# Preparing the second attention's first batch inside the layer before it, and another order for the first two token tiles of the last layer

## The reference, cut to what matters

```python
# second cross-attention: q from the normalised x, k and v from the context
attn = jnp.einsum('bct,bcs->bts', qh * scale, kh * scale)   # 8 heads of 64 channels
attn = jax.nn.softmax(attn, axis=-1)
out = jnp.einsum('bts,bcs->bct', attn, vh)
# FFN1: every operand is rounded to fp8 in blocks of 32 with one scale a block
gate = _mx_linear(x2d, gate_w); up = _mx_linear(x2d, up_w)
h = jax.nn.silu(gate) * up            # then rounded again, times down_w
```

## Time and profile before

| what | value |
|---|---|
| median of 3 runs | 1505.21 us (1503.46 to 1505.53) |
| the profiled execution | 1497.97 us |
| its span, first to last instruction | 1496.2 us |
| mean granted TensorE clock | 0.930 |
| PE busy | 1294.4 us (87%) |
| DVE busy | 1168.2 us (78%) |
| ACT busy | 659.3 us (44%) |
| POOL busy | 475.3 us (32%) |

### The profile page before, as it was taken

How to read it: one execution, slowest core, us unless ns; L and a number is a source line. 1 busy time by engine, 2 the same in 40 slices (tenths; PEclk the granted TensorE clock), 3 DMA queues, 4 the chain that set the end, 5 groups by cost and what they waited for, 6 DMA issues and landing times. The chain is left out here.

```text
span 1496.2 us, 20180 instructions
## 1 busy us (share of the span) xinstructions
PE 1294.4 (87%) x7472; PEld 649.8 (43%) x7496; DVE 1168.2 (78%) x1554; ACT 659.3 (44%) x1047; POOL 475.3 (32%) x344
## 2 busy tenths in 40 slices
PE   4589999466998899985787888889999999999998
PEld 3268777331444444442122222334444444444444
DVE  5557787875888788894868768788888878888885
ACT  3345666255554455433555545233343344433322
POOL 0031431365566566641458697200000000000000
PEclk8879999555999999998799999999999999999999
DMA  8412123237434252234001003130000000000000
GB/s 298 152 62 68 31 99 99 90 120 211 149 120 132 88 155 85 85 127 168 30 6 51 15 16 112 53 117 8 7 14 7 7 7 7 7 7 7 14 8 15
DMA packets 59734, 106.77 MB, mean 71 GB/s; under 512 B 10879, under 2 KB 21783, under 8 KB 59532
## 3 DMA queue, kind: packets, MB, share of 16 engines
q1 hardware_dynamic: 58380, 101.60, 21.0%
q0 software_dynamic: 1280, 4.20, 1.0%
HBM read 73.73 MB, written 27.66 MB: 68 GB/s over the span
## 5 line engine op out<-in xcount | busy, mean ns | idle before, releaser
L1697 PE MATMUL FD<-W0D,HH 128*128 128x512 f16 x512 | 156.2, 387 | 7.7 <-DVE ROOM L1756 3.4
L2597 PE MATMUL HD<-W1H,HT 128*128 128x512 f16 x480 | 145.2, 379 | 0.0
L335 ACT ACTIVATE DD<-E,TM 128x128 f32<-128x128 f32 x256 | 72.7, 369 | 69.6 <-PE E L431 68.0
L1691 PE MATMUL FG<-F,W0G 97*128 97x512 f16 x324 | 82.2, 384 | 20.8 <-PEq L1036 11.6
L1622 POOL TENSOR_TENSOR HL<-ROOM,HH 128x512 f16<-128x512 f32 x48 | 76.1, 1585 | 74.9 <-ACT HH L1651 74.9
L1697 PE MATMUL FD<-W0D,HL 128*128 128x512 f16 x256 | 98.8, 386 | 0.0
L2359 DVE TENSOR_REDUCE NQ<-A_M 128x2 f32<-128x1024 f32 x60 | 73.3, 1222 | 31.8 <-PE A_M L2204 31.5
L2156 ACT ACTIVATE PT<-A_S,CM 128x1024 f32<-128x1024 f32 x64 | 71.1, 1112 | 58.3 <-PE A_S L2230 58.1
L2597 PE MATMUL HD<-W1L,HT 128*128 128x512 f16 x240 | 91.0, 379 | 0.0
L2071 POOL TENSOR_TENSOR SS<-SS,PT 128x512 f32<-128x512 f32 x62 | 83.3, 1363 | 23.6 <-ACT PT L2156 17.6
L2516 ACT CAST OS<-SS 128x2048 f16<-128x2048 f32 x14 | 26.6, 1899 | 143.9 <-DVEq L2689 143.9
(11 more groups left out here) (407 smaller groups left out, 3062.0 us busy)
## 6 DMA issues: line engine op xcount, KB each, us to landing
VALP<-in_ffn_weights_dram SPq DMA_DIRECT2D x24, 512.0 KB, 4.2
VALQ<-in_ffn_weights_dram SPq DMA_DIRECT2D x24, 512.0 KB, 4.2
quantised_weights<-QQ SPq DMA_DIRECT2D x24, 512.0 KB, 2.7
X<-in_x_dram SPq DMA_DIRECT2D x8, 1024.0 KB, 6.4
W1H<-quantised_weights SPq DMA_DIRECT2D x3, 2048.0 KB, 9.4
F<-features_kept SPq DMA_DIRECT2D x16, 288.0 KB
CTX<-in_ctx_dram SPq DMA_DIRECT2D x4, 1024.0 KB, 7.0
features_kept<-XQ SPq DMA_DIRECT2D x4, 1024.0 KB, 7.1
```

The source lines that it names most:

```text
L335: ins = nc.scalar.activation(DD[:, n % 4, c * P:(c + 1) * P], E[n % 2][:, c * P:(c + 1) * P], ACT.Exp, bias=TM[:, 13 + c, b, h:h + 1])
L1691: last = pe.matmul(banks[t][:, :], GW[rows, t, lhs, cols], F[b % 2][rows, rhs, c, :], start=(n == 0), stop=(n == 2))
L1697: last = pe.matmul(DN[c][:, :], lhs[:, at, c * P:(c + 1) * P], W2[:, i, part, :], start=(i == 0 and n == 0), stop=(i == KI - 1 and n == 2))
L2597: ins = pe.matmul(DN[:, :], HT[:, q, lp, k, :], W[:, 2, i * D:(i + 1) * D], start=(i == 0 and lp == 0 and W is WH), stop=(i == KI - 1 and ...
```

## The change

1. `FirstBatch` prepares batch 0 of the attention inside FFN0. Its statistics come at stage 2, step 4, all else in stage 3 at the steps of `ENTRY`. The partition maximum is transposed to a row by TensorE (`columns`), reduced (`largest`) and spread by a product with ones (`everywhere`) in place of GpSimd's all-reduce. The statistics of batch 1 are taken there too.
2. The weight transposes of stage 3 come three steps after a tile's last chunk, not two.
3. Tiles share memory in another way: the FFN0 weights and features lie where the FFN1 weights come later, and the first part of these (`weights(0, 0)`) is loaded in group 3 of the attention, not at its start.
4. In the attention the preparation of batch 0 is gone, the low part before the scores too.
5. In FFN1 the order on VectorE and ScalarE for the first two tiles is another one, and in every stage TensorE's first gate product comes before the transposes of the hidden tile.

```diff
@@ rounding_plan
-        last = max(e + 2, last + 1)
+        last = max(e + (2 if e < (STAGES - 1) * STEPS else 3), last + 1)
@@ new class FirstBatch (cut)
+    def statistics(self, v, b):
+        if b == 0:
+            self.step(v, v.memset(self.EPS[:, :], 1e-5))
+            self.step(v, v.memset(self.ONER[:, :], 1.0))
+        for n in range(b * NC, (b + 1) * NC):
+            v.bn_stats(self.ST[:, n, :], self.X[:, n, :]).then_inc(self.st_ready, 1)
+        v.wait_ge(self.st_ready, (b + 1) * NC)
+        for n in range(b * NC, (b + 1) * NC):
+            v.bn_aggr(self.MV[:, n, :], self.ST[:, n, :]).then_inc(self.mv_ready, 1)
+    def columns(self, pe, bank):
+        pe.wait_ge(self.cm_ready, 1)
+        pe.wait_ge(self.vt_ready, NC)
+        pe.transpose(bank[0:1, 0:P], self.CM[:, 0, 0:1], self.idf).then_inc(self.cm_row, 1)
+    def largest(self, v, bank):
+        v.wait_ge(self.cm_row, 1)
+        v.tensor_reduce(self.TOP[:, :], bank[0:1, 0:P], AX.X, ALU.max).then_inc(self.top_ready, 1)
+    def everywhere(self, pe, bank):
+        pe.wait_ge(self.top_ready, 1)
+        pe.matmul(bank[:, 0:1], self.ONER[:, :], self.TOP[:, :], start=True, stop=True).then_inc(self.cm_all, 1)
...
+ENTRY = {"deviation": 0, "inverse": 1, "queries": 2, "high": 4, "low": 5, "turn": (7, 9), "values": (8, 10),
+         "top": 11, "columns": 12, "everywhere": 13, "keys": 14}
@@ ffn0_phase, VectorE
+                    if s == STAGES - 2 and i == 4:
+                        v.wait_ge(x_added, NC)
+                        entry.statistics(v, 0)
+                    if s == STAGES - 1:
+                        if i == ENTRY["inverse"]:
+                            entry.inverse(v, 0)
+                        if i == ENTRY["top"]:
+                            entry.top(v)
+                            entry.low(v)
+                            v.wait_ge(x_added, 2 * NC)
+                            entry.statistics(v, 1)
+                            entry.largest(v, GU[0])
+                        if i == STEPS - 2:
+                            entry.inverse(v, 1)
+                            entry.scale(v, GU[1])
+                            entry.keys_low(v)
@@ attention_phase, VectorE
-            statistics(0, range(NC))
-            inverse(0)
-            top(0, 0)
-            top(0, 1)
-            scale(0)
-            statistics(1, range(NC))
             for i in range(8):
                 slot(0, i)
-                if i == 2:
-                    inverse(1)
             negatives(0)
-            low(0, slice(0, NC))
@@ ffn1_phase, ScalarE
             first_silu(1, 0)
+            tokens.high(act, 2)
             first_silu(1, 1)
+            first_silu(1, 2)
+            tokens.turned(act, 2, 0, T[0][:, :, :, :])
             act.wait_ge(hv_ready, 1)
             nc.scalar.copy(HQ[:, 0, :], V[:, :]).then_inc(hh_ready, 1)
-            tokens.high(act, 2)
-            first_silu(1, 2)
-            tokens.turned(act, 2, 0, T[0][:, :, :, :])
             first_silu(1, 3)
@@ ffn1_phase, TensorE, stage
+                if gate_up:
+                    gate_up_products(tt, par, 0, 0)
                 if down:
                     turn_hidden(tt - 2, (0, 1))
                 if gate_up:
-                    for t in range(2):
-                        gate_up_products(tt, par, 0, t)
+                    gate_up_products(tt, par, 0, 1)
@@ ffn1_phase, VectorE, first_stages
                 next(second)
+                next(second)
                 gated(0, 0)
                 for _ in second:
                     pass
+                for q in range(2):
+                    norm.normalise(v, QUADS - 2, q)
                 tokens.moments(v, 2)
                 gated(0, 1)
                 parts = quant_first()
                 next(parts)
+                next(parts)
                 gated(0, 2)
-                for g in (QUADS - 2, QUADS - 1):
-                    for q in range(2):
-                        norm.normalise(v, g, q)
+                next(parts)
+                gated(0, 3)
                 prepared = tokens.prepare(v, 2)
                 next(prepared)
-                gated(0, 3)
+                gated(1, 0)
+                next(prepared)
+                for q in range(2):
+                    norm.normalise(v, QUADS - 1, q)
+                for _ in prepared:
+                    pass
+                next(parts)
+                gated(1, 1)
                 next(parts)
                 next(parts)
-                gated(1, 0)
                 next(parts)
-                next(parts)
-                gated(1, 1)
-                for _ in prepared:
-                    pass
                 gated(1, 2)
```

More of the change, by code:

```diff
@@ L1677, in _ @@
                         high(s + 1, i)
+                    else:
+                        if i == ENTRY["deviation"]:
+                            entry.deviation(act, 0)
+                        if i == ENTRY["queries"]:
+                            act.wait_ge(features.t_ready, B * KD)
+                            entry.queries(act)
+                        if i == ENTRY["high"]:
+                            act.wait_ge(u_ready, B * KI)
+                            entry.high(act)
+                        if i in ENTRY["values"]:
+                            for j in range(2):
+                                entry.values(act, 2 * ENTRY["values"].index(i) + j, GU[j])
+                        if i == ENTRY["keys"]:
+                            entry.deviation(act, 1)
+                            entry.keys(act)
         @block.tensor
@@ L1727, in _ @@
                             down(s, c, j)
+                        if i in ENTRY["turn"]:
+                            for j in range(2):
+                                pe.wait_ge(hm_ready, B * KI)
+                                entry.turn(pe, 2 * ENTRY["turn"].index(i) + j, GU[j])
+                        if i == ENTRY["columns"]:
+                            entry.columns(pe, GU[0])
+                        if i == ENTRY["everywhere"]:
+                            entry.everywhere(pe, GU[1])
                     if s + 2 < B:
@@ L2019, in _ @@
             context(1)
-            weights(0, 0)
             weights(0, 1)
             for g in range(QUADS):
+                if g == 3:
+                    sp.wait_ge(o_ready, NC * NC)
+                    weights(0, 0)
                 if g % 2 == 0 and 2 <= g // 2 + 2 < B:
@@ L2112, in queries @@
                 for c in cs:
-                    ins = nc.scalar.activation(XN[:, c, :], X[:, b * NC + c, :], ACT.Identity, scale=RS[:, c:c + 1],
-                                               bias=NB[:, c:c + 1])
+                    rs, nb = (t[:, NC + c:NC + c + 1] if b == 1 else u[:, c:c + 1] for t, u in ((entry.RS, RS), (entry.NB, NB)))
+                    ins = nc.scalar.activation(XN[:, c, :], X[:, b * NC + c, :], ACT.Identity, scale=rs, bias=nb)
                 if c == NC - 1:
@@ L2138, in _ @@
             act.wait_ge(consts, CONSTS + 1)
-            deviation(0)
-            queries(0, range(NC))
-            high(0, slice(0, NC))
-            keys(0, slice(0, NC))
-            for j in range(NC):
-                values(0, j, SB[j // 2][:, j % 2, :])
-            deviation(1)
             queries(1, range(NC))
@@ L2240, in weigh @@
                         pe.wait_ge(o_taken, pair)
+                vt = VT[:, b % 2, j, :] if b else entry.VT[:, j, :]
                 for par, r in enumerate(half):
-                    last = pe.matmul(OB[r, :], VT[:, b % 2, j, c * P + par * AC:c * P + (par + 1) * AC],
+                    last = pe.matmul(OB[r, :], vt[:, c * P + par * AC:c * P + (par + 1) * AC],
                                      PT[:, k % RING, par, :], start=(j == 0), stop=(j == NC - 1))
                 last.then_inc(o_ready, 1)
-            for j in range(NC):
-                turn(0, j, SB[j // 2][:, j % 2, :])
             pe.wait_ge(consts, CONSTS + 1)
-            largest(0, 0)
-            pe.wait_ge(vt_ready, NC)
-            for i in range(1, 8):
+            for i in range(8):
                 largest(0, i)
@@ L2908, in build_program @@
         ctx_in = [nc.alloc_semaphore(f"d_ctx{b}") for b in range(B)]
+        WH = top.enter_context(nc.sbuf_tensor("W1H", [P, 3, RUNS], F16))
+        WL = top.enter_context(nc.sbuf_tensor("W1L", [P, 3, RUNS], F16))
+        entry = FirstBatch(nc, X, TG, CST[:, 0:P], WH, WL, ROOM, ctx_in, top)
         with ExitStack() as weights:
-            GW = weights.enter_context(nc.sbuf_tensor("W0G", [P, 2, 2, INTER], F16))
-            W2 = weights.enter_context(nc.sbuf_tensor("W0D", [P, KI, 2, D], F16))
+            GW = WH[:, 0, :].rearrange("p (t a f) -> p t a f", t=2, a=2)
+            W2 = WH[:, 1:3, :].rearrange("p t (k a c) -> p (t k) a c", k=KI // 2, a=2)
             MV = weights.enter_context(nc.sbuf_tensor("MV0", [P, TILES, 2], F32))
@@ L2923, in build_program @@
```

(1 more changed line is left out.)

124 lines of the change are left out of this document (101 added, 23 removed).

## The result

| | before | after |
|---|---|---|
| median | 1505.37 us, 4 runs (1503.46 to 1507.07) | 1482.6 us, 4 runs (1477.18 to 1487.19) |
| ratio, 95% interval | | 0.9848 [0.9812, 0.9883] |
| profiled execution, span | 1497.97 us, 1496.2 us | 1483.21 us, 1481.4 us |
| mean granted clock | 0.930 | 0.934 |

22.8 us are gained, where 15.6 were forecast. The two profiled executions lie 14.8 us apart. By the ratio, the 1505.21 us that the prediction started from become 1482.3 us; the low end of its range was 1482.5 us.

A forecast was written before the change was run, and what follows sets the result against it. TensorE alone was taken to bound FFN1, with holes at the attention's start and FFN1's first tiles. Gains of 8.8 and 6.8 us gave 1482.4 us, with the 7.2 us median offset 1489.6 us; range 1482.5 to 1497 us.

The forecast's parts named there:

- Statistics in stage 2: FFN0 stage 2, VectorE: statistics, aggregations and two memsets delay all that follows by 3.2 us, bounds 0 to 4.
- The rival that hides them: FFN0 stage 2: TensorE's unused time hides the statistics, 3.2 us more gain, 1486.4 us; chance 0.14.
- End of FFN0: FFN0 stage 3: the last residual add comes 7.4 us later, 3.2 from stage 2, the rest from a serial tail.
- a gap behind the last down product: Sign at FFN0's end: a stretch of 5 to 8 us between the last down product and the first `largest`.
- The context load: FFN0 stage 3: issued at 663 instead of 651.3, landed at 669; TensorE waits 2 us, at no cost.
- The small instructions held beside GpSimd: Stage 3: a 128x32 VectorE instruction takes 1.157 us on average where GpSimd scales, 0.24 us alone.
- the large pass that I lengthened: Stage 3, VectorE's `low`: a pass such as the one of 2.29 us, plus 0.8 us for GpSimd's simultaneous work.
- First scores: Attention's start: first scores at 715.7 instead of 724.47, a gain of 8.8 us.
- FFN1's first tiles: FFN1's start: the new order brings the down products earlier, a gain of 6.8 us, bounds 2 and 10.
- Later stages: Every other FFN1 stage: the later hidden turn and ScalarE copies cause no wait, 0 us.
- The sum: Whole kernel: 8.8 + 6.8 = 15.6 us off the profiled 1497.97 us, giving 1482.4 us.
- the last line of the sum: Whole kernel: the runs' median lies 7.2 us above the profiled execution; taking this over gives 1489.6 us.

The follow-up runs named there:

- e2: The changed kernel, unchanged, timed again: 1479.4 us, 4 runs, ratio 0.9854 to the kernel before.
- e4: The changed kernel without its new FFN1 order, so with the attention's first batch prepared in FFN0 only: 1486.22 us, ratio 0.990.
- e6: The changed kernel with filler products on TensorE from the last down product to the first scores: 1486.06 us, ratio 0.987.
- e11: The changed kernel with TensorE's old order in each FFN1 stage, hidden transposes before the first gate product: 1486.61 us, ratio 0.9891.
- e1: The kernel before, unchanged, timed against itself: 1503.01 us, 12 runs, ratio 1.0001.
- e9: The kernel before with the three tiny VectorE instructions of inverse(1) after the first of eight maxima, not the third: 1499.3 us, ratio 0.9979.
- e10: The kernel before with inverse(1) after the fourth maximum, inside GpSimd's low pass: 1502.5 us, ratio 1.0002.
- e5: The kernel before with filler products on TensorE while it waits at the attention's start: 1502.0 us, ratio 0.9971.
- the first group: Follow-up kernels run on one chip: both kernels again and each half of the change alone; the kernel before had median 1502.70 us there.
- e7: The changed kernel with stage 3's tail reordered, row maximum and scale early, statistics of batch 1 last: 1479.92 us, ratio 0.984.
- e8: The changed kernel with GpSimd's all-reduce in FFN0's stage 3 in place of TensorE's transpose, row maximum and product with ones: 1488.29 us, ratio 0.9877.

## Why the prediction was wrong, point by point

Right in direction, and each term that the sum had came within about 1 us of its measurement; the size of the gain was 22.8 us and not 15.6.

*Statistics in stage 2*: forecast 3.2 us, the rows show 3.14. From FFN0's first add to its last gate product the profile of before has 156.0 us, after 159.1 and e2 160.1; the end of stage 2 comes 3.1 us later in both. The rival that hides them is out.

*End of FFN0*: forecast 7.4 us later, measured 6.25 us. From first to last add it is 219.9 us in all six profiles with the old FFN0 and 226.1 us in all five that have the new one as it stands (after, e2, e4, e6, e11). The two first profiles show 8.8 us, since 2.5 of these had arisen before the first add. So stage 3 cost 3.2 us and not the 4.2 that I gave it. The order of events was as forecast: `largest` last, `everywhere` waited for (2.30 us), a gap behind the last down product, though of 4.1 us where I had named 5 to 8. The context load was issued 2.3 us later than forecast, about what the draw explains, and cost TensorE the 2.08 us forecast. The small instructions held beside GpSimd were fewer: L1397 averages 895 ns over five in this stretch, not the 1157 of the earlier trace rows, and the large pass that I lengthened (`low`, 2.28 us) went through at full speed; it was GpSimd that was held, 3.80 us for a pass of 2.13, and nobody waited for it.

*First scores*: forecast gain 8.8 us. Counted from the first add they come after 250.0 us in the profile of before and 249.8 us in e1, and after 240.1 us in after and e2: 9.7 to 9.9 us. The surplus is FFN0's end, which came 1.1 us less late than forecast. From the last add to the scores 14.05 us were forecast (701.65 to 715.7) and 14.0 measured.

*FFN1's first tiles*: forecast 6.8 us; 7.3 us between the first two profiles, 5.8 us between e1 and e2, 6.5 us between the averages of all profiles (62.8 and 56.2 us, e11 left out). Its inner shape was less right: of TensorE's waits behind `gated` I gave 0.5 us and there are 3.8, since VectorE's list ran later than my sum; I had the first down products 7.3 us earlier by one route, and the profile took another of the same length. *Later stages*: 0 forecast, 0 measured.

*The sum*: 15.6 us forecast, 14.8 us between the two profiled executions. That the two agree so well is in part luck: the terms measured are 9.9 and 7.3 us, and 2.5 us went to the later first add, which is no effect of the change.

**The step that failed** is the last line of the sum: "The median of the runs shown is 1505.21, 7.2 us above that execution; I take the difference over to it". It takes the offset as a property of the measurement, equal for both kernels. e1 and e2 refute that: their profiles are 23.8 us apart and not 14.8. The offset was a draw of single executions, and parts of it are losses at places that the change removes or shortens, for which the sum has no term:

- the held instruction, about 3.6 us where it comes (18.1 and 18.3 us from `largest` to the scores against 14.5 and 14.6). That it costs time is shown by experiment (e9 against e10); in how many executions of before it comes is not.
- the score phase. The six profiles with the old entry average 210.9 us (208.9 to 213.7), the seven with the new one and no filler 208.1 us (205.5 to 209.2): 2.8 us, a term that my sum did not have; it had the entry as ended at the first scores. The windows of e1 and e2 from first scores on, cut where TensorE's clock comes back, show part of it (the columns are those of the earlier trace rows):

```profile
724.30:731.70 7.40, 7.37 (x28) 1.51 (x28) 5.43 (x11) 4.80 (x5) 0.38 (x1) 0.50 0.45 143
731.70:752.90 21.20, 16.39 (x92) 4.41 (x92) 17.31 (x19) 9.72 (x10) 17.23 (x13) 0.98 0.00 1
```

```profile
714.80:718.20 3.40, 3.40 (x16) 0.74 (x16) 1.41 (x7) 2.60 (x3) 0.38 (x1) 0.50 0.01 2
718.20:739.00 20.80, 17.79 (x102) 4.78 (x102) 16.57 (x18) 12.48 (x13) 14.41 (x11) 1.00 0.00 1
```

At 0.50, 1.2 GHz, TensorE works for 7.4 us of scores before and for 3.4 us after; the first group of eight score steps takes 28.3 us there and 24.5 us here. But e2 is the extreme case. Over all profiles the clock comes back 7.3 us after the first scores with the old entry (e5 left out) and 6.3 us with the new one, and the first group averages 28.0 and 26.8 us. The earlier trace rows had shown the clock of 0.60 in this hole, and I priced the hole and not what the clock takes with it into the next phase; by the profiles that is about 1.2 us. e6, whose low clock ends before the scores, has 23.1 us. This is shown by profiles and not by the times, which e6 did not better.

The other 1.6 us of the score phase lie where the code is the same in both kernels, 0.9 us of them in the third group (31.9 and 31.0 us on average), and can be a draw. What differs there between single executions is the granted clock. The third group of before, and that of e1, which is the same code:

```profile
779.80:810.40 30.60, 22.76 (x128) 5.75 (x128) 24.09 (x25) 14.29 (x15) 18.95 (x15) 0.94 0.17 52
```

```profile
779.90:814.10 34.20, 24.38 (x126) 6.28 (x124) 26.38 (x25) 14.29 (x15) 21.36 (x17) 0.85 0.16 47
```

The unfilled kernels have 3.4 us at 1.2 GHz in this group, and then it takes 30.0 to 30.6 us (seven profiles), or 10.2 us, and then it takes 31.8 to 34.2 us (five). Why an execution falls on one side or the other stays open.

Added up with terms free of the early draw: 9.8 (first scores) + 6.5 (FFN1) + 2.8 (score phase) = 19.1 us, and up to 3.6 us more for the held instruction, by how often it comes: 19.1 to 22.7 us. Measured are 22.8 us here, with an interval of 17.6 to 28.3 us, and 1502.70 - 1479.40 = 23.3 us in the first group, with 18.2 to 25.7 us. So these terms can make up the whole, and some us stay unassigned if the held instruction comes in only half of the executions. The range was cut by the same step: its low end, 1482.5 us, allowed the stage-2 rival and 2 us for the offset, where the 7.2 us themselves could be kept or vanish.

## What to carry to other kernels

When the profiled execution is clearly off the median of the runs, the difference is a term of the sum: take a second profile, ask which waits and low-clock stretches the usual execution has and this one lacks, and whether the change removes their place. Two engines that pass the same spot a few tenths of a us apart, as the inverse and GpSimd's low pass did here (0.2 us), are such a place. To compare two profiles, count from a landmark just ahead of the first changed instruction: here it took away a spread of 10 us, and from there to FFN0's last add the profiles of one code agree within 0.1 us. And where a change fills or shortens a hole in TensorE's work, price the clock after the hole too (about 1 us here); where an in-order engine meets a wait, look for one independent product to put ahead of it (4.0 us here).

## What the runs showed of the hardware

- A VectorE TENSOR_SCALAR over 128x4 elements is held 2.96, 3.42 and 3.94 us by a GpSimd pass of 4.04 us, to its very end, where it takes 0.17 us alone. A RECIPROCAL of the same size and maxima out of PSUM run through the same pass unhindered (0.17 and 1.21 us). The Trainium skill's page "SBUF — State Buffer" (section "SBUF: two separate sides") calls the shared port pair "an exclusive lock, not a bandwidth split", for GpSimd against VectorE's two-port mode or its instructions with two SBUF inputs. The trace agrees: the price is what is left of the other's pass, whatever the size of one's own.
- It goes the other way too: GpSimd's pass of 2.13 us took 3.80 us (after) and 4.44 us (e7) where VectorE's pass with two SBUF inputs, 2.27 us, fell into it, and VectorE's was not lengthened. The excess in e7 is 2.31 us, VectorE's whole pass, although GpSimd's is recorded as begun 0.19 us earlier (685.18, 685.37).
- GpSimd's partition maximum starts 5.9 us ("issue") after a pass in e8 and 10.1 to 10.6 us late at a block's start, and the pass after it again 8.0 to 8.8 us later, for 0.38 us of recorded work. What GpSimd does meanwhile no profile shows. Batch 1's maximum in the profile of before has no such delay: its input is done at 726.82 us, and it starts at 726.96.
